# Layer 0 of a two-layer graph network: gathered rows laid out anew, and their weighting and summing on VectorE regrouped

## The reference

```python
xs_e, xv_e = xs[src], xv[src]                 # rows gathered by edge
es, ev = edge_feat[:, 0], edge_feat[:, 1:4]   # four harmonics of an edge
out_s = (einsum('eu,uo->eo', xs_e * es[:, None], W_ss) / sqrt(64)
         + einsum('eud,ed,uo->eo', xv_e, ev, W_vv) * ISQ3 / sqrt(32)) * ISQ2
out_v = (einsum('eu,ed,uv->evd', xs_e, ev, W_sv) * ISQ3 / sqrt(64)
         + einsum('eud,e,uv->evd', xv_e, es, W_vs) * ISQ3 / sqrt(32)) * ISQ2
messages = concatenate([out_s, out_v]) * sigmoid(edge_scalars @ W_rad.T + b_rad)
agg = segment_sum(messages, dst)
```

## Time and profile before

| | before |
|---|---|
| median of 3 runs | 4367.61 us (4367.43 to 4368.17) |
| the profiled execution | 4365.39 us, its span 4363.6 us |
| granted TensorE clock, mean over the span | 0.789 |
| PE busy | 3885.0 us (89%) |
| DVE busy | 3885.0 us (89%) |
| POOL busy | 3137.4 us (72%) |
| ACT busy | 2657.9 us (61%) |
| DMA, mean | 147 GB/s |

### The profile page before, as it was taken

One profiled execution on the slowest core, in us unless ns is written; L12 is line 12 of the kernel. 1 busy time (PEld: TensorE's weight loads), 2 busy tenths in 40 slices (PEclk: granted clock), 3 DMA queues, 4 the chain that ended last, 5 costly groups with the idle time before them and its releaser, 6 DMA issues.

```text
span 4363.6 us, 64697 instructions
## 1 busy us (share of the span) xinstructions
PE 3885.0 (89%) x14024; PEld 2504.5 (57%) x14025; DVE 3885.0 (89%) x8520; ACT 2657.9 (61%) x8218; POOL 3137.4 (72%) x3268
## 2 busy tenths in 40 slices
PE   7898999989999898899878898899888888889887
PEld 5565666656666666666655555555555555555556
DVE  4999999999999999999768898988888998898997
ACT  5666666666666666666555566666656666666664
POOL 4777777777777777777457777777777777777771
PEclk7656555565555556655799999999999999999999
DMA  9666666666666666666333333333333333333332
GB/s 291 192 194 192 191 193 192 192 193 193 190 193 192 192 194 191 190 194 192 113 99 102 102 100 102 104 103 102 103 99 101 103 103 103 104 102 103 104 104 60
DMA packets 245760, 640.04 MB, mean 147 GB/s; under 512 B 57101, under 2 KB 95439, under 8 KB 245627
## 3 DMA queue, kind: packets, MB, share of 16 engines
q0 software_dynamic: 181136, 556.56, 46.5%
q1 hardware_dynamic: 64592, 83.11, 6.1%
HBM read 618.56 MB, written 20.88 MB: 147 GB/s over the span
## 4 chain that ended last, share of the span: by engine, by line
DVE 52%; PE 16%; issue 15%; DVEq 6%; DMA 4%; ACT 3%; POOL 2%; SPq 0%; POOLq 0%; ACTq 0%
PE ps L1005 11%; DVE work L702 10%; DVE onehot L746 10%; DVE work L676 7%; DVE arena L754 4%; DVE work L726 3%; DVE work L669 3%; DMA arena<-table,srcs 3%; DVE work L723 2%; DVE work L689 2%; DVEq L811 2%; DVE acc L754 2%; ACT work L487 2%; PE ps L982 2%; POOL arena L390 2%
## 5 line engine op out<-in xcount | busy, mean ns | idle before, releaser
L390 POOL DMA_INDIRECT arena<-table,srcs x1596 | 1544.0, 967 | 486.2 <-issue 432.9
L390 POOL DMA_INDIRECT work<-table,srcs x1596 | 1523.0, 954 | 500.4 <-issue 482.7
L1005 PE MATMUL ps<-work,onehot 128*128 128x384 f32 x3608 | 1311.6, 510 | 224.6 <-DVE work L733 130.3
L487 ACT ACTIVATE work<-arena,harm 128x160 f32<-128x160 f32 (+1 forms) x3224 | 985.4, 388 | 452.6 <-DMA arena<-table,srcs 435.6
L1005 PE MATMUL ps<-arena,onehot 128*128 128x161 f32 x3608 | 1020.4, 459 | 198.9 <-DVE arena L712 167.4
L1005 PEld LDWEIGHTS ps<-arena,onehot 128*128 128x128 f32 x3608 | 872.8, 305 | 513.8 <-issue 440.6
L487 ACT ACTIVATE work<-work,harm 128x96 f32<-128x96 f32 (+1 forms) x3224 | 1071.4, 415 | 121.4 <-DMA work<-table,srcs 63.1
L1005 PEld LDWEIGHTS ps<-work,onehot 128*128 128x128 f32 x3608 | 671.1, 195 | 775.2 <-issue 328.4
L982 PE MATMUL ps<-wrad,escal 49*128 49x320 f32 x1612 | 890.1, 697 | 0.0
L746 DVE SCALAR_TENSOR_TENSOR onehot<-ps,bases,dst_sh 128x512 f32<-128x512 f32 x902 | 670.8, 744 | 14.6 <-DVE acc L754 7.3
L702 DVE TENSOR_REDUCE work<-work 128x256 f32<-128x768 f32 (+1 forms) x806 | 654.1, 851 | 0.7 <-ACT ps L515 0.4
(11 more groups left out here) (131 smaller groups left out, 2222.4 us busy)
## 6 DMA issues: line engine op xcount, KB each, us to landing
escal<-in_escal SPq DMA_DIRECT2D x404, 98.0 KB
arena<-table,srcs POOLq DMA_INDIRECT x1596, 3.5
work<-table,srcs POOLq DMA_INDIRECT x1596
table<-work SPq DMA_DIRECT2D x49, 224.0 KB, 6.1
dst_sh<-in_dst_sh SPq DMA_DIRECT2D x52, 160.0 KB, 3.2
table<-work SPq DMA_DIRECT2D x7, 784.0 KB, 4.0
acc<-in_xd SPq DMA_DIRECT2D x1, 3920.0 KB, 22.4
arena<-in_xd SPq DMA_DIRECT2D x7, 560.0 KB, 4.3
```

The lines of the kernel that those rows point to most:

```text
L390: pool.indirect_dma_start(out=rows[:, j, t, :], out_offset=None, in_=table, in_offset=bass.IndirectOffsetOnAxis(ap=of[:, j, t:t + 1], axis ...
L487: last = nc.scalar.activation(u[:, t, to:to + c1 - c0], r[:, t, c0:c1], ACT.Copy, scale=harm[:, j, at:at + 1])
L1005: last = mm(bank(to)[:, 0:(MSG0, MSG1)[l]], onehot[:, b, t, :], m[:, j % 2, t, :], start=t == 0, stop=t == TPS - 1)
```

## The change

The 448 columns of a table row are put in another order, so that the columns that DVE multiplies lie together: 0 to 191 (harmonics 1 and 2, 96 columns each), 192 to 287 (harmonic 0, ACT), 288 to 447 (harmonic 3, ACT). The order of the rows of `xT` and of the blocks in `w0a` and `w0b` follows; the scaling pieces are one fewer on ACT.

At the first slot of a round DVE copies the round's harmonics from `dst_sh` into bank 7 of PSUM (`harm0`). It waits for the gathered rows itself, and no longer for ACT. One product 128 x 768 (4 tiles, 2 harmonics, 96 columns) takes the place of the product of L669 and the four instructions of L676. The two reductions are replaced by three additions: the four scalar parts in pairs (4 x 2 x 64 elements, both operands in `weighted0`), the vector parts (4 x 3 x 32), and, behind the wait for the sigmoid, the two pair sums (4 x 64). The wait for all of ACT's weighting before `select` stays, and stands once more before the first addition; the wait for the sums two supertiles back (`s_agg`) stays in front of the add (L754). The message product (L712), ACT's instructions in the loop (other columns, same sizes), PE and POOL's gathers keep their form.

```diff
+        harm0 = hps[:, 0:4 * TPS * SLOTS].rearrange("p (j c) -> p j c", j=SLOTS)
...
-        SCALED0 = [(w0a[0:64, 128:192], I8 * ISQ2), (w0a[0:64, 0:128], I8 * ISQ3 * ISQ2), (w0a[0:64, 192:448], I8 * ISQ3 * ISQ2),
+        SCALED0 = [(w0a[0:64, 384:448], I8 * ISQ2), (w0a[0:64, 0:384], I8 * ISQ3 * ISQ2),
...
-                weight(u, r, 3, 96, 256, 128, j % PAIR).then_inc(s_whead, 1)
-                weight(u, r, 0, 256, 352, 288).then_inc(s_wtd[0], 1)
+                weight(u, r, 3, 288, 448, 64, j % PAIR)
+                weight(u, r, 0, 192, 288, 224).then_inc(s_wtd[0], 1)
...
                 if l == 0:
-                    dve.wait_ge(s_whead, s + 1)
+                    if j == 0:
+                        nc.vector.tensor_copy(harm0, of_round(i, slice(0, SLOTS), slice(TPS, 5 * TPS)).bitcast(f32)).then_inc(s_harmp[0], 1)
+                        dve.wait_ge(s_harmp[0], i + 1)
+                    dve.wait_ge(s_rows[0][j], (i + 1) * 16 * TPS)
                     u, r = weighted0[:, j % DEEP0, :, :], rows0[:, j, :, :]
-                    nc.vector.tensor_tensor(u[:, :, 384:480], r[:, :, 352:448], by(1), ALU.mult)
-                    for t in range(TPS):
-                        if t == 1:
-                            dve.wait_ge(s_add[0], s + 1)
-                        if t == TPS - 1 and not opens:
-                            dve.wait_ge(s_agg[0], s + 1)
-                        to = u[:, t, 128:224]
-                        last = nc.vector.scalar_tensor_tensor(to, r[:, t, 0:96], harm[:, j, 4 * t + 2:4 * t + 3], to,
-                                                              ALU.mult, ALU.add)
-                    last.then_inc(s_wone[0], 1)
+                    nc.vector.tensor_tensor(u[:, :, 320:512].rearrange("p t (k c) -> p t k c", k=2),
+                                            r[:, :, 0:192].rearrange("p t (k c) -> p t k c", k=2),
+                                            bc(harm0[:, j, :].rearrange("p (t k) -> p t k", k=4)[:, :, 1:3], 3, [P, TPS, 2, 96]),
+                                            ALU.mult).then_inc(s_wone[0], 1)
+                    if not opens:
+                        dve.wait_ge(s_agg[0], s + 1)
...
-                summed(u[:, :, 0:MS], 160, 3)
+                dve.wait_ge(s_wtd[0], s + 1)
+                parts = u[:, :, 160:544].rearrange("p t (k c) -> p t k c", k=4)[:, :, :, 0:MS]
+                nc.vector.tensor_tensor(parts[:, :, 0:2, :], parts[:, :, 0:2, :], parts[:, :, 2:4, :], ALU.add).then_inc(s_pairs, 1)
+                vectors = u[:, :, MS:DIM].rearrange("p t (k c) -> p t k c", k=3)
+                nc.vector.tensor_tensor(vectors, vectors, u[:, :, 224:512].rearrange("p t (k c) -> p t k c", k=3)[:, :, :, 0:MV],
+                                        ALU.add)
                 dve.wait_ge(s_act[0], s + 1)
-                summed(u[:, :, MS:2 * MS], 224, 2).then_inc(s_part[0], 1)
+                dve.wait_ge(s_pairs, s + 1)
+                nc.vector.tensor_tensor(u[:, :, 0:MS], parts[:, :, 0, :], parts[:, :, 1, :], ALU.add).then_inc(s_part[0], 1)
                 dve.wait_ge(s_part[0], s + 1)
...
-                mm(p[:, 32:128], x1[:, of_tile], w0b[:], start=False, stop=True).then_inc(s_tmm, 1)
+                mm(p[:, 224:320], x1[:, of_tile], w0b[:], start=False, stop=True).then_inc(s_tmm, 1)
```

More of the change, by code:

```diff
@@ L204, in mk_gnn_resnorm_d2_gnn_r8_694f30_kernel @@
         s_harmp = [sem(f"harmonics_in_psum{l}") for l in range(2)]
-        s_whead = sem("scalar_parts_weighted")
         s_wone = [sem(f"rows_weighted_by_dve{l}") for l in range(2)]
+        s_pairs = sem("scalar_parts_paired")
         s_part = [sem(f"message_part{l}") for l in range(2)]
@@ L445, in _ @@
             act.wait_ge(s_w0, 32)
-            for w, c in SCALED0[:3]:
+            for w, c in SCALED0[:2]:
                 nc.scalar.activation(w, w, ACT.Copy, scale=c).then_inc(s_w0scaled, 1)
@@ L624, in _ @@
                     dve.wait_ge(s_w0, 32)
-                    for w, c in SCALED0[3:]:
+                    for w, c in SCALED0[2:]:
                         nc.vector.tensor_scalar(w, w, c, None, ALU.mult).then_inc(s_w0scaled, 1)
@@ L661, in weight_by_one @@
             def weight_by_one(l, s, i, j, opens):
-                def by(k):
-                    return harm[:, j, :].rearrange("p (t k) -> p t k", k=4)[:, :, k:k + 1].to_broadcast([P, TPS, 96])
                 if l == 0:
-                    dve.wait_ge(s_whead, s + 1)
+                    if j == 0:
+                        nc.vector.tensor_copy(harm0, of_round(i, slice(0, SLOTS), slice(TPS, 5 * TPS)).bitcast(f32)).then_inc(s_harmp[0], 1)
+                        dve.wait_ge(s_harmp[0], i + 1)
+                    dve.wait_ge(s_rows[0][j], (i + 1) * 16 * TPS)
                     u, r = weighted0[:, j % DEEP0, :, :], rows0[:, j, :, :]
-                    nc.vector.tensor_tensor(u[:, :, 384:480], r[:, :, 352:448], by(1), ALU.mult)
-                    for t in range(TPS):
-                        if t == 1:
-                            dve.wait_ge(s_add[0], s + 1)
-                        if t == TPS - 1 and not opens:
-                            dve.wait_ge(s_agg[0], s + 1)
-                        to = u[:, t, 128:224]
-                        last = nc.vector.scalar_tensor_tensor(to, r[:, t, 0:96], harm[:, j, 4 * t + 2:4 * t + 3], to,
-                                                              ALU.mult, ALU.add)
-                    last.then_inc(s_wone[0], 1)
+                    nc.vector.tensor_tensor(u[:, :, 320:512].rearrange("p t (k c) -> p t k c", k=2),
[4 more added lines that the diff above has]
+                        dve.wait_ge(s_agg[0], s + 1)
                 else:
@@ L697, in messages0 @@
                 dve.wait_ge(s_wone[0], s + 1)
-                def summed(to, at, k):
-                    parts = u[:, :, at:at + k * P].rearrange("p t (k c) -> p t k c", k=k)
-                    return nc.vector.tensor_reduce(to, parts[:, :, :, 0:MS].rearrange("p t k c -> p t c k"), AX.X, ALU.add)
                 def by_half(x):
                     return x.rearrange("p (h k) c -> p h k c", h=2)
-                summed(u[:, :, 0:MS], 160, 3)
+                dve.wait_ge(s_wtd[0], s + 1)
[4 more added lines that the diff above has]
+                                        ALU.add)
                 dve.wait_ge(s_act[0], s + 1)
-                summed(u[:, :, MS:2 * MS], 224, 2).then_inc(s_part[0], 1)
+                dve.wait_ge(s_pairs, s + 1)
+                nc.vector.tensor_tensor(u[:, :, 0:MS], parts[:, :, 0, :], parts[:, :, 1, :], ALU.add).then_inc(s_part[0], 1)
                 dve.wait_ge(s_part[0], s + 1)
@@ L1206 @@
     by_component = np.concatenate([s_of, *v_of])
+    v_of_kept = [MS + MV * d + np.arange(MV) for d in range(3)]
     xd = placed(NODES_PAD, DIM, (0, 0, x[:, by_component]))
@@ L1230 @@
     ins = {
-        "xT": xd.T, "xd": xd,
+        "xT": xd.T[np.concatenate([s_of, *(v_of_kept[d] for d in (1, 2, 0))])], "xd": xd,
         "srcs": np.concatenate([by_supertile(src, 0).transpose(1, 0, 2), np.zeros((P, SLOTS, TPS), src.dtype)], axis=1),
@@ L1237 @@
         "attr": placed(NODES_PAD, 1, (0, 0, attr)).reshape(NODE_TILES, P).T,
-        "w0a": placed(P, ROW0, (0, 0, wsv), (0, 128, wss), (64, 192, wvs), (96, 224, wvs),
-                      (64, 256, wvv), (0, 320, wsv), (0, 352, wsv), (96, 384, wvv)),
+        "w0a": placed(P, ROW0, (0, 0, wsv), (64, 32, wvv), (0, 96, wsv), (96, 128, wvv), (0, 192, wsv),
+                      (64, 320, wvs), (96, 352, wvs), (0, 384, wss)),
         "w0b": placed(P, 96, (0, 0, wvv), (0, 64, wvs)),
```

## The result

| | before | changed | 
|---|---|---|
| median | 4367.89 us (4367.43 to 4375.35, 4 runs) | 4400.4 us (4397.05 to 4406.23, 4 runs) |
| ratio to the kernel before | | 1.0071, 95% interval 1.0059 to 1.0083 |
| span of the profiled execution | 4363.6 us | 4396.9 us |
| mean gather in layer 0, 150 to 2050 us | 967 ns | 984 ns |
| mean gather in layer 1 | 954 ns | 954 ns |

What follows compares the result with a forecast made beforehand. The prediction took POOL's queue of gathers to bound layer 0. Profiled span 4363.6 + 40 (gather stretch) - 2 (loop end) = 4401.6, plus 4.0 from span to median = 4405.6, said as 4406 us; range 4345 to 4450.

Steps and rivals of the forecast that it cites:

- The bound: Layer 0's loop: POOL's queue of gathers sets the time, 0.305 us idle a gather, no wait over 0.3 us.
- (a): DVE work removed in layer 0: L669, four L676 and two L702, 3.04 us a supertile.
- (b): DVE work added in layer 0: one product and three additions, 2.42 us; DVE falls to 4.06 us a supertile.
- (c): Layer 0: the DVE saving, 0.62 us x 403 = 250 us, is worth nothing by itself.
- (d): Layer 0: two-SBUF additions stretch gathers by 0.185 us a supertile against 0.085 before, +40 us.
- the chance of meeting: Layer 0: gather starts fall evenly over DVE's two-SBUF blocks; pairs cost 0.104, vectors 0.057, last 0.024 us a supertile.
- the first rival: Layer 0: additions keep a fixed place after a landing; vectors met, 0.125 us, 4382 (chance 0.11), or faster (0.14).
- its check by layer 1: Layer 1: one two-SBUF instruction, 0.006 us a supertile, so mean gather (954 ns) within 2 ns of an undisturbed one.
- (e): Layer 0's waits: a message comes 5.5 us after its rows land, hidden behind POOL, cost 0.
- (f): End of layer 0's loop: the last message comes at 2119.0 in place of 2120.68, -2 us.
- The sum: Whole kernel: 4363.6 + 40 - 2 = 4401.6, plus 4.0 from span to median, 4406 us.
- The rule weighed: Two-SBUF DVE instructions and SBUF-reading GpSimd ones exclude each other for the first's whole length; 4851 us, under 1 in 100.

Runs made afterwards that it cites:

- experiment 8: Kernel of experiment 2 with a copy of 416 elements a partition (0.52 us) ahead of its additions; 4427.13 us, ratio 1.0136.
- experiment 9: Kernel of experiment 2 with a copy of 160 elements a partition (0.25 us) ahead of its additions; 4333.42 us, ratio 0.992.
- experiment 2: Changed kernel, complete, with harmonic 1's product and the scalar sums in PSUM, two short two-SBUF additions left; 4326.96 us, ratio 0.9902.
- experiment 5: Kernel before, with the second operand of L669 and the four L676 from a PSUM constant (output incomplete); 4342.25 us, ratio 0.9948.
- experiment 3: Changed kernel with a copy of 160 elements a partition ahead of the three additions, about 0.25 us later; 4408.17 us, ratio 1.0088.
- experiment 6: Changed kernel with a copy of 416 elements a partition ahead of the additions, about 0.52 us later; 4404.0 us, ratio 1.0079.
- experiment 1: Changed kernel with the second operand of all three additions from a PSUM constant (output incomplete); 4335.02 us, ratio 0.992.
- experiment 4: Changed kernel with the copied harmonics in SBUF in place of PSUM, so the product has two SBUF operands; 4495.03 us, ratio 1.0281.
- experiment 10: Changed kernel with the second operand of the pairs' addition alone from a PSUM constant (output incomplete); 4384.53 us, ratio 1.0032.

## Why the prediction was right, point by point

**The bound.** Right. POOL's gathers come 0.305 us behind each other before and after, with no longer wait. Experiments 8 and 9 show it from the other side, on the kernel of experiment 2: 0.25 us of DVE work a supertile costs nothing that can be measured, 0.52 brings the bound to DVE.

**(a), (b) DVE's new work.** Right: 4.06 us a supertile forecast; the timeline has 4.01 from one L670 to the next (1002.29 to 1006.30), with 0.60 + 0.47 + 0.45 + 0.74 for the three additions and L710, and durations within 5 ns of the estimates. DVE's busy share is 82%, as said.

**(c) The saving is worth nothing by itself.** Right for the changed kernel. The step has a limit it didn't state: by the prediction's own count the kernel before was 0.04 us a supertile from being bound by DVE (20.2 against 20.34 us a round), and without the stretch it is (experiment 5).

**(d) The stretch.** The mechanism was right, the size too large: 0.185 us a supertile forecast, 4 x (984 - 947) = 0.148 measured, +40 us forecast and 27 measured. The term that was mis-sized is the chance of meeting. By chance pairs cost 38 us in the window, vectors 21, last 9; counted in the trace they cost 18, 35 and 5. So the gathers' starts don't fall evenly: they fall into the vectors more often than into the pairs, as the first rival had it (0.125 us a supertile); the measured value lies between the two. Shifting them gave 0.212 and 0.188 us (experiments 3 and 6, 1000 and 994 ns). Chance gives the middle of these three, 0.18, not the single value; the first rival's arithmetic for its direction failed in experiment 3. What sets the place, a landing as the rival had it or something else, was not worked out and stays open. Three smaller things in this step: in experiments 1 and 5, where nothing stretches, the mean gather is 945 ns and not 947, which puts the stretch at 0.09 before and 0.16 after and leaves the growth as it is. The time under two-operand instructions goes, by the prediction's own pitches, from 0.48 + 0.91 = 1.39 to 0.61 + 0.48 + 0.45 = 1.54 us, not from 1.46 to 1.57; the sum doesn't use it. And its check by layer 1 was no check as it stood: 954 is 7 ns above 947, where 2 were allowed. The trace mends it: half of layer 1's gathers take 953 ns or less and only 24 of 1596 take over 990, so an undisturbed gather is longer there, and the mean lies 1 ns above it.

**(e) Waits.** As said: the wait for ACT in front of L744 is there (207 us), and the wait for the sigmoid before the last addition is 0.4 us in all. PE waits somewhat longer for the one-hot product (44.6 us against 27.3), but POOL waits for nobody, and POOL is the bound.

**(f) The end of the loop.** Right: from the start of layer 0's last gather to that of layer 1's first it is 126.3 us before and 124.9 after, -1.4 where -2 was forecast.

**The sum.** In the profiled executions the span grew by 33.3 us: +27.7 from the first to the last gather of layer 0, -0.2 before the first, -1.4 in between, +3.3 in layer 1's gathers and +3.9 behind them. The last two were taken as unchanged, and no changed line runs there; the last section has what is known of layer 1, and the 3.9 us behind it stay unexplained. So the total came nearer the forecast (33 of 38) than the loop did (28 of 40), and by that much it is luck.

**The rule weighed** (the Trainium skill, SBUF — State Buffer, section "SBUF: two separate sides"). By these runs the exclusion exists and needs two SBUF operands on DVE's side (experiments 1, 4, 5), as the page says. But a gather doesn't hold off DVE for its whole length: the additions at 1005.11 (0.42 us) and 1009.01 (0.68) run inside gathers at their usual length. Only an addition that already runs when a gather starts, and ends more than 0.13 us later, changes anything.

## What to carry to other kernels

Where POOL issues indirect DMAs back to back and they set the time, look at their mean duration and at which DVE instructions have two operands in SBUF: each such instruction of D us costs about (D - 0.175)² / (2 x 1.25) us on average (0.175 is 0.13 us and the 0.045 of the prediction, 1.25 the time from one gather to the next). Summed over the three blocks that came out within 20% (0.148, 0.212 and 0.188 for 0.185, in the changed kernel and experiments 3 and 6), for two of them at 1.4 times the price (experiment 10); a single block can cost half of it or twice as much, by where it falls (the pairs 18 us for 38 in the changed kernel, 71 for 36 in experiment 4). By the square one long one is worse than several short ones, and with one operand in PSUM it stretches nothing. A DVE saving beside such a queue counts only up to the point where DVE's whole round, loop ends and rare visits included, is shorter than the bound's; add these before saying that an engine has slack.

## What the runs showed that was not expected

Layer 1, which no experiment touches, isn't of constant length. From its first gather to its last it took 2042.3 us in the kernel before, 2045.6 in the changed one, 2052.6 in experiment 1, 2035.4 in experiment 2 and 2033.0 in experiment 5: a spread of 20 us, more than half of the effect under study. It goes with TensorE's granted clock. In experiment 1, PE (timeline) stood still for 2.55 us until 3094.81 and then did 16 matmuls in 8.50 us; a little later 8 of the same take 2.85 us, where 16 had needed 8.50:

```profile
3094.81 8.50 PE L1007 MATMUL ps<-work,onehot 128*128 128x384 f32 x16 [2.55 <-DVE onehot L746]
...
3104.51 2.85 PE L1007 MATMUL ps<-work,onehot 128*128 128x384 f32 x8
```

The stretch around it has a granted clock of 0.71, a mean of its two levels of 1.2 and 2.4 GHz; in the trace the lower one holds from 3094 us for 6.8 us:

```profile
3090.00:3100.00 10.00, 7.45 (x22) 4.04 (x21) 9.04 (x21) 4.14 (x12) 7.56 (x9) 0.71 0.35 98
```

POOL, which waits there for messages at the end of a long way, then stands idle for 3.15 us in place of 0.30:

```profile
3105.94 0.95 POOL L393 DMA_INDIRECT work<-table,srcs  x1 [3.15 <-issue]
```

Over layer 1 the clock was at 1.2 GHz for 126 us in experiment 1, 106 in the changed kernel, 96 before, 82 in experiment 2 and 72 in experiment 5, which is the order of the five lengths. In the other seven traces 102 and 109 us go with 2049 and 2047 us, and 75 to 89 with 2032 to 2038. That the clock brings about the length is argued from the one place above; no run changed the clock by itself. So a difference of 10 us between two kernels here needs the loop itself, gather by gather, and not the total. That is where part of experiment 2's gain comes from: of its 38.3 us of span against the kernel before, 31 lie in layer 0's loop, 7 in layer 1.
